# A cross-attention kernel on one core: query products issued ahead of the value products in every step

## The reference

```python
q = heads(hidden_states @ W_q)
k_t = heads(text_ehs @ W_k)
v_t = heads(text_ehs @ W_v)
probs_t = softmax(einsum('bhsd,bhtd->bhst', q, k_t) * attn_scale)
text_out = einsum('bhst,bhtd->bhsd', probs_t, v_t)
attn_scores = einsum('bhsd,bhnd->bhsn', q, k_ip) * attn_scale
qsem = l2norm(einsum('bhst,bte->bhse', probs_t, text_ehs))
sem = einsum('bhse,bne->bhsn', qsem, l2norm(ip_ehs))
probs_ip = softmax(attn_scores + SEM_SCALE * sem) * spatial_mask
ip_out = einsum('bhsn,bhnd->bhsd', probs_ip, v_ip)
out = (text_out + ip_out) @ W_out + b_out + residual
```

## Time and profile before

| | |
|---|---|
| median of 3 runs | 1023.91 us (1021.89 to 1025.69) |
| the profiled execution | 1022.47 us |
| its span, first to last instruction | 1020.6 us |
| mean granted TensorE clock | 0.988 |
| TensorE matmuls | 969.2 us busy, 95% |
| TensorE weight loads | 803.6 us, 79% |
| VectorE | 816.6 us, 80% |
| ScalarE | 695.6 us, 68% |
| GpSimd | 655.2 us, 64% |
| chain that ended last | TensorE 77% of the span, DMA 5%, VectorE 4% |

### The profile page before, as it was taken

The page is one execution under the profiler, slowest core; times in us unless marked ns, Lnnn a source line. Parts: engine busy times, 40 slices in busy tenths (PEclk is TensorE's granted clock), DMA queues, the critical chain, the costliest instruction groups (busy, mean ns, idle before and its releaser), DMA issues.

```text
span 1020.6 us, 24929 instructions
## 1 busy us (share of the span) xinstructions
PE 969.2 (95%) x7684; PEld 803.6 (79%) x7684; DVE 816.6 (80%) x2409; ACT 695.6 (68%) x2332; POOL 655.2 (64%) x1906
## 2 busy tenths in 40 slices
PE   5987788999999999999999999999999999999988
PEld 5875666888878888888887888888878888888855
DVE  6685698888888887888888888878878888878872
ACT  3534887777776777767776777777667777777740
POOL 3224587776676667677766777676667767776761
PEclk9978999999999999999999999999999999999999
DMA  9936999989889998899899989998899989887973
GB/s 293 298 117 161 195 179 186 177 163 180 168 186 186 186 185 177 163 176 162 174 178 192 192 164 191 169 167 173 167 190 187 180 169 190 137 157 154 149 138 111
DMA packets 488147, 180.27 MB, mean 177 GB/s; under 512 B 449694, under 2 KB 467155, under 8 KB 488015
## 3 DMA queue, kind: packets, MB, share of 16 engines
q1 hardware_dynamic: 487983, 178.63, 86.3%
q10 hardware_dynamic: 32, 0.07, 0.0%
HBM read 42.34 MB, written 27.22 MB: 68 GB/s over the span
## 4 chain that ended last, share of the span: by engine, by line
PE 77%; DMA 5%; DVE 4%; ACT 2%; issue 2%; SPq 2%; POOL 1%; DVEq 0%; ACTq 0%; POOLq 0%
PE ps_O L1257 25%; PE ps_Q L1368 25%; PE ps_S L1278 12%; PE ps_U L1354 11%; DMA pts<-ph 4%; PE ps_M L1294 3%; ACT pr L1038 2%; DMA x_in<-in_x_dram 1%; SPq L951 1%; DVE pr L1199 0%; PE ps_U L1257 0%; DVE n L1211 0%; ACT ph L1050 0%; DVE bias L1160 0%; SPq L924 0%
## 5 line engine op out<-in xcount | busy, mean ns | idle before, releaser
L1038 ACT ACTIVATE pr<-ps_S,bias 128x73 f32<-128x73 f32 x1280 | 288.8, 339 | 101.3 <-DVE bias L1160 100.1
L1120 POOL TENSOR_TENSOR ph<-pr,ph 128x220 f16<-128x220 f32 (+1 forms) x640 | 274.0, 460 | 126.2 <-ACT ph L1050 126.2
L1368 PE MATMUL ps_Q<-xT,wq_hi 128*128 128x512 f32 x800 | 280.1, 415 | 5.2 <-DVE qT L1127 5.2
L1257 PE MATMUL ps_O<-wo_hi,aT 128*128 128x320 f16 x1220 | 279.2, 300 | 0.0
L1050 ACT ACTIVATE ph<-pr 128x292 f16<-128x292 f32 x640 | 241.2, 500 | 0.0
L1257 PE MATMUL ps_O<-wo_lo,aT 128*128 128x320 f16 x610 | 182.3, 299 | 0.0
L1354 PE MATMUL ps_U<-xm,pts 128*128 128x110 f16 (+1 forms) x2560 | 159.3, 212 | 14.9 <-DMA pts<-ph 13.5
L1368 PEld LDWEIGHTS ps_Q<-xT,wq_hi 128*128 128x128 f32 x800 | 146.2, 191 | 32.7 <-DVE qT L1127 6.5
L1354 PEld LDWEIGHTS ps_U<-xm,pts 128*128 128x128 f16 (+1 forms) x2560 | 144.4, 98 | 32.3 <-issue 11.8
L1278 PE MATMUL ps_S<-kbd,qT 128*128 128x308 f32 x960 | 163.0, 304 | 2.6 <-ACT pr L1038 2.1
L1278 PEld LDWEIGHTS ps_S<-kbd,qT 128*128 128x128 f32 x960 | 150.8, 188 | 18.6 <-issue 3.0
(11 more groups left out here) (228 smaller groups left out, 1338.9 us busy)
## 6 DMA issues: line engine op xcount, KB each, us to landing
out_dram<-x_in SPq DMA_DIRECT2D x64, 320.0 KB, 2.6
x_in<-in_x_dram SPq DMA_DIRECT2D x56, 320.0 KB, 3.2
pts<-ph SPq DMA_TRANSPOSE x320, 3.4
w_k<-in_L_xattn_W_k_dram SPq DMA_DIRECT2D x5, 512.0 KB, 8.8
w_ip<-in_L_xattn_W_k_ip_dram SPq DMA_DIRECT2D x1, 2560.0 KB, 11.0
w_v<-in_L_xattn_W_v_dram SPq DMA_DIRECT2D x5, 512.0 KB, 8.3
w_ip<-in_L_xattn_W_v_ip_dram SPq DMA_DIRECT2D x1, 2560.0 KB, 10.6
x_in<-in_x_dram SPq DMA_DIRECT2D x2, 1280.0 KB, 7.2
```

The lines of the kernel that those rows point to most:

```text
L1038: last = nc.scalar.activation(pr[p % P_RING][:, j, h, :], sc[:, j, h, 0:T], ACT.Exp, bias=bias[p % 2][:, j, h:h + 1], scale=SCALE)
L1120: nc.gpsimd.tensor_tensor(lo, full[:, :, t0:t1], one[:, :, 0, t0:t1], ALU.subtract).then_inc(pl_ready, 1)
L1257: last = nc.tensor.matmul(bank[:, 0:HALF], stationary, moving, start=(k, a, b_) == O_MMS[0], stop=(k, a, b_) == O_MMS[-1])
L1368: last = nc.tensor.matmul(ps_Q[:], wq[a][:, c, k * P:(k + 1) * P], xT[(CC * i + c) % XT_RING][b_][:], start=(c, a, b_) == Q_MMS[0], stop=( ...
```

## The change

In TensorE's program the block that issues Q moves ahead of the block that issues U, in every step. The wait for q_lo moves with it. Nothing else is touched, on no other engine.

```diff
@@ -1336,6 +1336,21 @@
                     if part == 3:
                         last.then_inc(o_ready, 1)
 
+                if q_at(p) is not None:
+
+                    m, part = q_at(p)
+                    i, k = divmod(m, CC)
+                    mms = Q_PARTS[part]
+                    if part == 0 and m:
+                        pe.wait_ge(q_lo, m)
+                    for c, a, b_ in mms:
+                        if k == 0 and (a, b_) == PASSES[0]:
+                            pe.wait_ge(xT_lo, CC * i + c + 1)
+                        last = nc.tensor.matmul(ps_Q[:], wq[a][:, c, k * P:(k + 1) * P], xT[(CC * i + c) % XT_RING][b_][:],
+                                                start=(c, a, b_) == Q_MMS[0], stop=(c, a, b_) == Q_MMS[-1])
+                    if part == 1:
+                        last.then_inc(q_ready, 1)
+
                 u = pair_of(p - LU)
                 if u is not None:
...
-                if q_at(p) is not None:
-
-                    m, part = q_at(p)
...
-                    if part == 1:
-                        last.then_inc(q_ready, 1)
-
```

## The result

The changed kernel takes 1154.93 us (median of 4 runs, 1153.39 to 1160.87), the kernel before, on the same chip, 1024.61 (1021.89 to 1025.69). The ratio is 1.129 [1.126, 1.133]. The forecast was 1129.6 with a range to 1152: the direction and the mechanism of the ring held, the size was 25 us too small, 3 us outside the range. The profiled execution took 1153.39 us, its span 1151.6 against 1020.6: 131.0 us more, where +107 had been forecast.

A forecast was written before the change was run, and what follows sets the result against it. TensorE was taken to set the pace from step 16 on. The closed ring's 103.2 us plus 9.9 early minus a credit of 6 gave +107 on 1022.5: 1129.6 us, range 1100 to 1152.

The forecast's parts named there:

- the ring: Main loop: odd-step Q waits for q_lo, queued behind VectorE's work on the last U; 103.2 us over steps 17 to 155.
- The credit of 6: TensorE's U: later U finds its operands ready, saving 6 us of the 13.5 us wait for pts.
- A: Path from odd-step U to the next through VectorE's even work and q_lo: 9.10 + G(even) + 0.46 per addition, in us.
- D: Path from odd-step U to the next through VectorE's odd work and ScalarE: 11.85 us, 11.39 without the output addition.
- the ring's term 0.87: VectorE's maximum plus copy plus bias ahead of the low part of the query: 0.87 us.
- Chunk 4: Step 8 of each tile: Q's last three products wait for VectorE's low part of a transposed chunk, 1.57 us.
- Rival 2: Step 8: the transposed chunk's low part comes in time, 23 us less, 1107 us; chance 12%.
- its term of +9.9: Early loop, steps 4 to 16 without output products: ScalarE path binds, 69.8 us instead of 59.9.
- rival 3: TensorE's clock: loop runs at granted clock 0.83, 118 us more, 1248 us; chance 2%.
- Waits of S for ScalarE instead: Sign of a wrong forecast: TensorE's S waits because the ring closes through exponentials; no size given.
- The rule against the change: Q's single bank: rotate banks, else each evacuation is exposed, 76 x (0.64 + 0.68) = 100 us; the ring was kept.

The follow-up runs named there:

- both_short: The changed kernel with GpSimd's low parts of attn and of ph both made only 4 columns wide: 1140.83 us, 1.116 to the kernel before.
- fill: The changed kernel plus ten unused products ahead of Q in odd steps 3 to 15: 1149.12 us, 1.125 to the kernel before.
- at_short: The changed kernel with GpSimd's low part of attn made on 4 of 128 columns only: 1150.82 us, 1.125 to the kernel before.
- the two-bank kernel: The changed order without transposes in the loop, Q alternating between banks ps_Q and ps_M: 1055.81 us, 1.035 to the kernel before.
- pool_order: The changed kernel with GpSimd's low part of attn moved behind its low parts of ph: 1175.88 us, 1.152 to the kernel before.

## Why the prediction was right or wrong

**What goes.** TensorE's wait for pts is gone,'s 13.5 us to nothing. The credit of 6 was 8.8 in the full part, within the ends of 0 and 13.5, but not for the reason given: from 200 us on the kernel before has only 4.0 us of waits for pts and 1.4 for x. For the rest of the 8.8, all in tiles near a change of batch, I have no row.

**The closed ring.** It is there as drawn: low part of the query, 0.05 us, Q, U, VectorE's work on U, and so on, with 79 waits where some 75 were forecast. The form of the sum was right, its size wasn't. The measured pairs against the larger of A and D:

| pair to step | forecast | measured | without the collisions (both_short) |
|---|---|---|---|
| 5 | 12.73 | 12.76 | 13.01 (one is left) |
| 7 | 11.85 | 12.07 | 11.77 |
| 9 | 13.92 | 14.28 | 13.89 |
| 1 | 12.02 | 12.46 | 12.07 |
| 3 | 12.35 | 12.46 | 12.39 |

**The step that failed** is the ring's term 0.87, "maximum plus copy plus bias", and beside it the 3.25 of the odd work on U in path D. Both came from rows in which GpSimd was hardly in the way. The 0.87 was read in an even step (514.50 to 515.37), but the term stands for an odd one, and there the bias was longer already in the kernel before: 0.38 us in step 5, right ahead of the low part that the earlier trace rows shows, and with a median of 0.29 in steps 7 and 9.

```profile
508.45 0.38 DVE L1160 TENSOR_SCALAR bias<-smax 128x8 f32<-128x8 f32 x1
```

In the new order the bias of steps 9 and 1 lasts 0.56 instead of 0.17, that of step 3 0.25, and w_sem 0.52 instead of 0.23 in four of the five odd steps. The pairs to 9, 1 and 3, which go by A, are 0.36, 0.44 and 0.11 above the forecast, by the bias. The pair to 7, which goes by D, is 0.22 above, by w_sem. Together the five pairs are 1.16 us a tile above the forecast, 16 us over 14 tiles. I had put a longer odd work on U into the range, and nothing for the bias.

The groups of the kernel before would have told that the price exists:

```profile
L1160 DVE TENSOR_SCALAR bias<-smax 128x8 f32<-128x8 f32 x160 | 41.3, 258 | 0.0
...
L1206 DVE TENSOR_TENSOR f<-nd,w_sem 128x64 f32<-128x64 f32 x80 | 25.1, 314 | 0.0
...
L1194 DVE SCALAR_TENSOR_TENSOR w_sem<-rd,inv,y 128x16 f32<-128x16 f32 x80 | 19.8, 247 | 3.0 <-POOL pip L1109 3.0
```

The bias has a mean of 258 ns and its shortest rows 170: it was held up before, too, in VectorE's slack, where it cost nothing. After the change:

```profile
L1160 DVE TENSOR_SCALAR bias<-smax 128x8 f32<-128x8 f32 x160 | 41.9, 262 | 0.0
...
L1194 DVE SCALAR_TENSOR_TENSOR w_sem<-rd,inv,y 128x16 f32<-128x16 f32 x80 | 35.9, 448 | 3.0 <-POOL pip L1109 3.0
...
L1206 DVE TENSOR_TENSOR f<-nd,w_sem 128x64 f32<-128x64 f32 x80 | 14.4, 180 | 0.0
```

The sum of the three is nearly unchanged (86.2 and 92.2 us); which of them is hit, and whether it lies on the path, has changed.

**Chunk 4.** Right: 15 waits, 1.52 us in the full part by the starts where 1.57 were forecast. Rival 2 is out.

**The early part** was 8.0 us above its term of +9.9, and p = 0 to 4, for which I had no term, 2.6. The second step that failed is here: the clock was put at nothing. This is rival 3, to which I gave 2%, in a small form: I had asked whether the whole loop would run at 0.83, not whether its emptiest twelfth would. By fill the clock is at least 5.5 of the 10.6. The rows of the changed kernel give more:

```profile
146.76 0.73 PE L1349 MATMUL ps_Q<-xT,wq_hi 128*128 128x512 f32 x2 [2.33 <-DVE xT L1127]
...
153.38 1.22 PE L1349 MATMUL ps_Q<-xT,wq_hi 128*128 128x512 f32 x2 [2.84 <-DVE qT L1127]
...
156.54 1.69 PE L1369 MATMUL ps_U<-xm,pts 128*128 128x110 f16 x16
```

The seven products of Q in p = 9 take 3.16 us (153.38 to 156.54), those of p = 79 take 1.74 (603.89 to 605.63), and U takes 1.69 instead of 0.99. Between 151.00 and 153.30, while TensorE stood, the granted clock was 0.50 already. Pair by pair, against the 11.39 of the forecast (from U of one odd step to U of the next):

| pair to p | above the forecast | slow Q and U | other |
|---|---|---|---|
| 5 | -0.9 | 0 | |
| 7 | 1.7 | 1.4 | |
| 9 | 2.9 (chunk 4's 1.5 taken off) | 1.6 | bias of 1.01 us: 0.8; chunk 4: 1.1 |
| 11 | 0.7 | 0.7 | |
| 13 | 1.0 | 1.0 | |
| 15 | 1.9 | 1.9 | |

The column of Q and U is what these instructions take beyond 1.74 and 1.02 us; that all of it lies on the path is an estimate, but in the last three rows it is the whole excess. The six pairs are 7.4 us above the forecast (8.0 by starts of S), and the lower level is some 6.7 of that, and 1.5 of the 2.6 before it, in p = 3. In p = 8 Q takes 4.54 us for 1.95, 2.6 of standing for chunk 4 where 1.5 had been added; it does the same in fill, so this is not the clock, and its cause stays open. The kernels at_short and both_short are slower early (about 80 us, clock 0.83 and 0.76 to 0.78) in the same way: their Q is slow in p = 5 and 11 too, 2.7 to 3.1 us.

**The other signs.** TensorE is 89% busy, not 86: its busy time has grown from 969.2 to 1020.9 us at the same number of matmuls. The records of S alone cover 30 us more (163.0 to 193.3), those of Q with wq_hi 8 (280.1 to 288.5). "Waits of S for ScalarE instead" was listed as a sign of a wrong ring; 48 are there besides those for qT. It is the second ring of the two-bank kernel; by its terms (8.89 and G(odd) with transposes: 12.06 to steps 5, 9 and 3, 11.68 to 7 and 1) it is 0.2 to 0.7 us shorter than the forecast's ring, chunk 4 apart.

**The rule against the change.** Each evacuation exposed gives 100 us, the ring 107, measured were 131 by spans. A second bank, which the rule asks for, brought 65.5 of 121: the bank was half of it. The other half is the order itself. U late means that VectorE's maximum is late, and with it the exponentials and the next S, with two banks as with one.

## What to carry to other kernels

Before moving a product ahead of another, write down who consumes each and what that consumer has in its queue behind it: the product moved back starts the long tail of another engine, and that tail, not the wait moved along, sets the new period. Then add every ring up, with and without the buffer in dispute, since a second buffer opens one of them only. Durations of instructions in an engine's slack are to be taken with their spread, and from the very steps that the term stands for, not from one clean row elsewhere: where the clean row and the mean of the group differ, look for what holds them up, since on the path it is paid.

## What the hardware showed that I had not expected

- **Some small VectorE instructions last until a running GpSimd instruction ends.** Bias (128x8) 0.17 us alone, 0.56 and 1.02 beside GpSimd; w_sem (128x16) 0.23 and 0.52; f (128x64) 0.17 and 0.74. In the 15 traces 1582 records of bias, w_sem, f, n2h and y are more than 0.1 us longer than undisturbed ones, and every one of them ends 0.02 to 0.09 us after a GpSimd instruction. It is not the size: reductions and reciprocals of the same small tiles (fmx, rd), begun while a low part of ph or attn had at least 0.3 us to run on GpSimd (121 and 159 cases), never took more than 0.21 and 0.20. Nor did VectorE's instructions that read PSUM, which took their usual 0.76 and 0.75. The kernel both_short, in which GpSimd's two instructions are narrow, has w_sem at 0.23 everywhere. The Trainium skill (SBUF — State Buffer, section Who interferes with whom) says that a VectorE instruction with two inputs in SBUF contends with a GpSimd instruction that reads SBUF, that one in a mode which uses both of VectorE's ports contends with GpSimd too, and that the one issued first has the shared ports for its whole length while the other waits. The trace agrees: w_sem and f have two inputs in SBUF; that the bias, with one, is held by its mode no run here shows.
- **A held-up instruction can be moved but not always removed.** pool_order brought the bias of steps 9 and 1 to 0.17 and 0.19 and lost 21 us against the change, 14 of them in the tiles, where f took the hit (0.74 behind the U of steps 9, 3 and 5).
- **TensorE's clock fell in the stretch with the least work.** Early it stood up to 2.84 us in an odd step and was granted 0.88 and 0.80; later, with waits of up to 1.3 us and O between, 1.00. At the lower level seven products of 512 columns took 3.16 us instead of 1.74. Products without use brought 0.97 and 0.93 and some 5.5 us. The Trainium skill (TensorE: Matmul & The Clock Gate, section on psum-queue depth-cycling) says that short idling between groups which cycle through PSUM can make the clock swing between its levels. In the kernel before the trace spoke against it; in the early part of the changed kernel it agrees.
